# Another order of VectorE's work, and the row maxima split on GpSimd, in a fused attention and FFN kernel

## The reference

```
x  = x + tanh(g_xattn) * attention(layernorm(x), ctx, ctx)      # 16 heads of 16, causal, softmax
x  = x + tanh(g_ffn)   * ffn(layernorm(x))

ffn(t): prob = softmax(t @ w_router + b_router)                 # 16 blocks
        mask = the 4 largest of the 16
        h    = relu(t @ w1.T + b1)                              # 1024 hidden, 64 to a block
        y    = sum over blocks of mask * (h @ w2.T) + b2
```

## Time and profile before

| | |
|---|---|
| median of 3 runs | 725.55 us (723.66 to 728.48) |
| the profiled execution's own time | 723.54 us |
| its span, first to last instruction | 721.8 us |
| busy: TensorE, its weight loads | 686.2 us (95%), 628.9 us (87%) |
| busy: VectorE, ScalarE, GpSimd | 576.3 us (80%), 514.2 us (71%), 512.2 us (71%) |
| iterations 6 to 61 (72.5 to 665.0 us of the span) | 592.5 us |

### The profile page before, as it was taken

One profiled execution on the slowest core, in us unless ns is written; L12 is line 12 of the kernel. 1 busy time (PEld: TensorE's weight loads), 2 busy tenths in 40 slices (PEclk: granted clock), 3 DMA queues, 4 the chain that ended last, 5 costly groups with the idle time before them and its releaser, 6 DMA issues.

```text
span 721.8 us, 30666 instructions
## 1 busy us (share of the span) xinstructions
PE 686.2 (95%) x13072; PEld 628.9 (87%) x13072; DVE 576.3 (80%) x1614; ACT 514.2 (71%) x785; POOL 512.2 (71%) x651
## 2 busy tenths in 40 slices
PE   6869999999999999999999999999999999999888
PEld 5657889998999999889899998989989899899787
DVE  5789988888887888888788888879888888977562
ACT  3656787787777778778777877877787786787532
POOL 3676767778777777877877787777777777765542
PEclk8979999999999999999999999999999999999999
DMA  5313354454345435435544443553454345242010
GB/s 163 99 42 61 75 109 87 86 109 91 77 98 108 89 87 108 86 70 109 108 80 95 109 75 88 102 109 76 98 105 74 88 109 87 59 79 47 20 37 30
DMA packets 161815, 61.91 MB, mean 86 GB/s; under 512 B 135696, under 2 KB 161424, under 8 KB 161680
## 3 DMA queue, kind: packets, MB, share of 16 engines
q1 hardware_dynamic: 160848, 58.38, 38.8%
q10 hardware_dynamic: 832, 1.57, 0.7%
HBM read 19.03 MB, written 8.39 MB: 38 GB/s over the span
## 4 chain that ended last, share of the span: by engine, by line
PE 61%; DVE 24%; issue 5%; ACT 4%; DMA 3%; POOL 2%; SPq 1%; POOLq 0%; ACTq 0%; DVEq 0%
PE bank L414 8%; PE bank L437 6%; PE score_banks L335 6%; PE bank L439 6%; PE bank L438 6%; PE bank L415 6%; PE bank L416 6%; PE score_banks L305 5%; PE bank L348 4%; DVE max_found_in L638 4%; PE bank L362 3%; DVE stats L608 3%; DVE hid L711 2%; DVE q_parts L651 2%; DVE x L666 2%
## 5 line engine op out<-in xcount | busy, mean ns | idle before, releaser
L832 POOL TENSOR_TENSOR h_low<-hid,h_high 128x512 fp32r<-128x512 f32 x128 | 165.2, 1291 | 118.6 <-ACT hid L532 118.4
L825 POOL TENSOR_SCALAR_AFFINE_SELECT weights<-weights 128x1024 f32<-128x1024 f32 x128 | 139.7, 1115 | 56.6 <-ACT weights L510 56.6
L414 PE MATMUL bank<-xT_high,w_high 128*128 128x256 f32 x496 | 151.1, 305 | 8.7 <-DVE hid L711 8.1
L510 ACT ACTIVATE weights<-score_banks 128x1024 f32<-128x1024 f32 x128 | 124.3, 1024 | 45.3 <-PE score_banks L335 45.3
L437 PE MATMUL bank<-w_high,h_high 128*128 128x256 f32 x488 | 142.0, 291 | 4.9 <-DVE y_out L689 4.3
L415 PE MATMUL bank<-xT_low,w_high 128*128 128x256 f32 x496 | 138.8, 280 | 0.0
L416 PE MATMUL bank<-xT_high,w_low 128*128 128x256 f32 x496 | 138.6, 279 | 0.0
L711 DVE SCALAR_TENSOR_TENSOR hid<-bank,b_cols,used_all 128x256 f32<-128x256 f32 x248 | 108.2, 477 | 36.9 <-PE bank L416 36.2
L439 PE MATMUL bank<-w_high,h_low 128*128 128x256 f32 x488 | 136.4, 280 | 0.0
L438 PE MATMUL bank<-w_low,h_high 128*128 128x256 f32 x488 | 136.3, 279 | 0.0
L414 PEld LDWEIGHTS bank<-xT_high,w_high 128*128 128x128 f32 x496 | 93.4, 188 | 19.4 <-DVE hid L711 14.0
(11 more groups left out here) (106 smaller groups left out, 1485.8 us busy)
## 6 DMA issues: line engine op xcount, KB each, us to landing
x_in<-in_x SPq DMA_DIRECT2D x31, 256.0 KB, 3.1
out_y<-y_out SPq DMA_DIRECT2D x31, 256.0 KB, 2.5
c_in<-in_ctx SPq DMA_DIRECT2D x30, 256.0 KB, 3.1
qT<-qT SPq DMA_DIRECT2D x128, 4.0 KB
w_stage<-in_w1T ACTq DMA_DIRECT2D x1, 1024.0 KB, 5.2
hid<-in_w2T SPq DMA_DIRECT2D x8, 128.0 KB, 2.6
kT_parts<-k_parts SPq DMA_TRANSPOSE x57, 3.3
qT_parts<-q_parts SPq DMA_TRANSPOSE x57, 3.3
```

The source lines that it names most:

```text
L414: pe.matmul(out=bank, lhsT=w1_high[:, k, c], rhs=high, start=k == 0, stop=False)
L510: act.activation(weights[:, b % 2, half * 2 * HB:(half + 1) * 2 * HB, :].rearrange("p h q -> p (h q)"), score_banks[:, 2 * half:2 * half + ...
L825: pool.affine_select(out=w, in_=w, compare_op=ALU.is_ge, fill=0.0, base=0, pattern=[[0, 2 * HB], [1, S]], channel_multiplier=-1).then_inc( ...
L832: pool.tensor_tensor(h_low[:, p % 2, chunks], hid[:, n % 4], h_high[:, p % 2, chunks].bitcast(F32), ALU.subtract).then_inc(h_low_made, 1)
```

## The change

- VectorE's order in an iteration: `finished` now ahead of `attention_added`; the mask of the first hidden piece right behind `row_maximum`, ahead of `normalised_again` and `layernorm_stats`.
- The maxima always go to column 20 of `q_pad`. `maximum_parts` on VectorE is gone; GpSimd's `query_parts` copies columns 0 to 20 in place of 0 to 15, waits for the maxima, and runs for the last two carriers too.
- GpSimd's `query_parts` stands behind `key_parts` and the first layernorm's rstd, where it was ahead of both.
- The addition of eps moves from VectorE to GpSimd, twice an iteration, in front of the power.
- SyncE: `max_row` ahead of `used_spread`.
- The three level columns of the high halves are no longer set to constants in `q_parts`; they are copied with the rest.

```diff
             def row_maximum(b):
                 dve.wait_ge(scored, b + 1)
                 carrier = b + MAX_LAG
-                ride = q_pad[:, carrier % QS, :, RIDE_COL] if q_early(carrier) else max_found_in[:]
-                ride = ride.rearrange("p (t g u) -> p u t g", g=2, u=U)
+                if carrier >= N:
+                    dve.wait_ge(q_parts_made, carrier - QS - QUERIES_BY_PE + 1)
+                ride = q_pad[:, carrier % QS, :, RIDE_COL].rearrange("p (t g u) -> p u t g", g=2, u=U)
...
-            def maximum_parts(b):
-                carrier = b + MAX_LAG
-                n, slot = divmod(carrier - QUERIES_BY_PE, 2)
-                dve.wait_ge(max_found, b + 1)
...
-                dve.tensor_copy(q_parts[:, slot, :, :, RIDE_COL],
-                                max_found_in[:].bitcast(U16).rearrange("p (h l) -> p l h", l=2)).then_inc(max_parts_made, 1)
...
             for i in ITERATIONS:                                  # VectorE
                 pr, pu = router_pair(i), used_pair(i)
                 p, m = hidden_pair(i)
+                if 0 <= i - OUT_LAG - 1 < N:
+                    finished(i - OUT_LAG - 1)
                 if 0 <= i - 2 < N:
                     attention_added(i - 2)
-                if 0 <= i - OUT_LAG - 1 < N:
-                    finished(i - OUT_LAG - 1)
                 if 0 <= i + 1 < N:
                     row_maximum(i + 1)
-                    if not q_early(i + 1 + MAX_LAG):
-                        maximum_parts(i + 1)
+                if p is not None:
+                    hidden_masked(p, m)
                 if 0 <= i - 2 < N:
                     normalised_again(i - 2)
                 if 0 <= i + 4 < N:
                     layernorm_stats(i + 4)
-                if p is not None:
-                    hidden_masked(p, m)
...
-            def rstd_of(ve, result, s, b, ve_made, rstd_made):    # GpSimd
+            def rstd_of(mv, ve, result, s, b, mean_made, ve_made, rstd_made):
+                pool.wait_ge(mean_made, b + 1)
+                pool.tensor_scalar(ve[:, s], mv[:, s, 1:2], LN_EPS, None, ALU.add).then_inc(ve_made, 1)
                 pool.wait_ge(ve_made, b + 1)
                 pool.tensor_tensor(result[:, s], ve[:, s], half_power[:], ALU.pow).then_inc(rstd_made, 1)
...
             def query_parts(b):
                 n, slot = divmod(b - QUERIES_BY_PE, 2)
-                pool.wait_ge(qn_made, b + 1)
+                if b < N:
+                    pool.wait_ge(qn_made, b + 1)
+                pool.wait_ge(max_found, b - MAX_LAG + 1)
                 if n >= 1:
                     pool.wait_ge(q_spread[slot], 16 * n)
-                pool.tensor_copy(q_parts[:, slot, :, :, 0:HD],
-                                 q_pad[:, b % QS, :, 0:HD].bitcast(U16).rearrange("p h (d l) -> p l h d", l=2)
+                pool.tensor_copy(q_parts[:, slot, :, :, 0:RIDE_COL + 1],
+                                 q_pad[:, b % QS, :, 0:RIDE_COL + 1].bitcast(U16).rearrange("p h (d l) -> p l h d", l=2)
                                  ).then_inc(q_parts_made, 1)
...
                 elif 0 < i + 3 < N:
                     values(i + 3)
-                if QUERIES_BY_PE <= i + 3 < N:
-                    query_parts(i + 3)
                 if KEYS_BY_PE <= i + 3 < N:
                     key_parts(i + 3)
                 if 0 <= i + 4 < N:
                     if i + 4 == 0:
                         pool.wait_ge(numbers_set, 1)
-                    rstd_of(ve1, rstd1, (i + 4) % 2, i + 4, ve1_made, rstd1_made)
+                    rstd_of(mv1, ve1, rstd1, (i + 4) % 2, i + 4, x_mean, ve1_made, rstd1_made)
+                if QUERIES_BY_PE <= i + 3 < N + MAX_LAG:
+                    query_parts(i + 3)
                 if 0 <= i < N:
                     causal_weights(i)
...
             for i in ITERATIONS:                                  # SyncE
                 pu = used_pair(i)
+                if 0 <= i < N:
+                    max_row(i)
                 if pu is not None:
                     used_spread(pu)
-                if 0 <= i < N:
-                    max_row(i)
                 if QUERIES_BY_PE <= i + 3 < N + MAX_LAG:
                     queries_spread(i + 3)
```

More of the change, by code:

```diff
@@ L30 @@
 ONE_HIGH = 0x3F80
-NEG_HIGH = 0xFC80
 LOAD_AHEAD = 6
@@ L112, in build @@
         kT = sb("kT", [P, TS, BANK], F32)
-        max_found_in = sb("max_found_in", [P, HEADS], F32)
         q_parts = sb("q_parts", [P, 2, 2, HEADS, PAD], U16)
@@ L180, in build @@
         x2_stats, x2_mean, xn_made = sem("x2_stats"), sem("x2_mean"), sem("xn_made")
-        ve1_made, ve2_made, max_parts_made = sem("ve1_made"), sem("ve2_made"), sem("max_parts_made")
+        ve1_made, ve2_made = sem("ve1_made"), sem("ve2_made")
         xT_low_made, hid_made, y_made = (sem(n) for n in ("xT_low_made", "hid_made", "y_made"))
@@ L196, in build @@
             "parts_zeroed", "parts_ones_set", "parts_levels_set", "k_parts_made"))
-        q_parts_zeroed, q_parts_ready, q_parts_made = (sem(n) for n in (
-            "q_parts_zeroed", "q_parts_ready", "q_parts_made"))
+        q_parts_zeroed, q_parts_made = sem("q_parts_zeroed"), sem("q_parts_made")
         w_low_made, h_low_made = sem("w_low_made"), sem("h_low_made")
@@ L605, in places, with stats_of @@
                                 ident16[rows, rows].unsqueeze(1).to_broadcast([PAD, U, PAD])).then_inc(place_made, 1)
-            def stats_of(source, stats, mv, ve, s, b, stats_made, mean_made, ve_made):
+            def stats_of(source, stats, mv, s, b, stats_made, mean_made):
                 dve.bn_stats(stats[:, s, :], source).then_inc(stats_made, 1)
@@ L610, in stats_of @@
                 dve.bn_aggr(mv[:, s, :], stats[:, s, :]).then_inc(mean_made, 1)
-                dve.wait_ge(mean_made, b + 1)
-                dve.tensor_scalar(ve[:, s], mv[:, s, 1:2], LN_EPS, None, ALU.add).then_inc(ve_made, 1)
             def layernorm_stats(b):
@@ L619, in layernorm_stats @@
                     dve.wait_ge(x_landed[slot], 16 * (n + 1))
-                stats_of(x_in[:, b % XS, :], stats1, mv1, ve1, b % 2, b, x_stats, x_mean, ve1_made)
+                stats_of(x_in[:, b % XS, :], stats1, mv1, b % 2, b, x_stats, x_mean)
             def normalised(b):
@@ L668, in attention_added @@
                 dve.wait_ge(x2_made, b + 1)
-                stats_of(x2[:, s], stats2, mv2, ve2, s, b, x2_stats, x2_mean, ve2_made)
+                stats_of(x2[:, s], stats2, mv2, s, b, x2_stats, x2_mean)
             def normalised_again(b):
@@ L864, in _ @@
                     b = i - 2
-                    rstd_of(ve2, rstd2, b % 2, b, ve2_made, rstd2_made)
+                    rstd_of(mv2, ve2, rstd2, b % 2, b, x2_mean, ve2_made, rstd2_made)
                     if b == 0:
@@ L890, in _ @@
                                     ).then_inc(parts_levels_set, 1)
[L891 to L895, removed]
+                    pool.memset(q_parts[:, :, :, :, RIDE_COL + 1:], 0).then_inc(q_parts_zeroed, 1)
                 if p is not None:
@@ L928, in queries_spread @@
                     sync.wait_ge(q_copied, b - 1)
-                if b < N:
-                    sync.wait_ge(q_parts_made, b - QUERIES_BY_PE + 1)
-                sync.wait_ge(max_parts_made, b - QUERIES_BY_PE + 1)
+                else:
+                    sync.wait_ge(q_parts_zeroed, 1)
+                sync.wait_ge(q_parts_made, b - QUERIES_BY_PE + 1)
                 sync.dma_start_transpose(qT_parts[:, slot].rearrange("p l (r s) -> p (l r) s", s=S),
```

## The result

The changed kernel takes 796.03 us (793.95 to 798.09, 4 runs) against 725.85: ratio 1.0965, 95% interval 1.0916 to 1.1015. The prediction was 796. Its profiled execution took 798.09 us with a span of 796.2.

What follows compares the result with a forecast made beforehand. TensorE was taken to set the pace at 10.58 us an iteration; the change makes a loop through GpSimd, SyncE and ScalarE 6.78 + 1.74 + 3.5 = 12.02 us. Over 53 turns 76 us, less 3: 796 us, range 758 to 832.

Steps and rivals of the forecast that it cites:

- the circle: GpSimd's query split, SyncE's transpose, ScalarE's join and last Relu, GpSimd's L832, next split: 12.02 us a turn against 10.58.
- The signs: Expected profile marks: ScalarE waits before the join 1 to 2 us each, 60 to 100 in all; TensorE idle some 15%.
- The terms: GpSimd work entering the stretch from L832 to the query transpose: 0.57 + 0.52 + 0.17 + 0.48 = 1.74 us.
- Key split: GpSimd's splitting of the keys, now ahead of the query split: 0.57 us more in each turn.
- power: GpSimd's operation for rstd1, now ahead of the query split: 0.52 us more in each turn.
- The copy: GpSimd's query split copying 21 columns for 16: 0.17 us more, low end 0.13.
- The additions: Two epsilon additions moved to GpSimd: 0.24 us each, 0.48 for both, ends 0.2 and 1.2.
- fixed part: Time from one query split to the next less the transfer: 6.78 us before plus 1.74, constant near 8.5.
- the transfer's: Landing of the queries' transpose, from its issue to ScalarE's join: mean put at 3.5 us, shortest taken as 3.0.
- SyncE's queue and the mask: Maxima's transfers ahead of the choice's transpose: worth 5.8 us of TensorE's waits; later choice holds the mask under 1 us.
- VectorE's order: Mask starts about 2.4 us earlier, xn behind it has room: worth TensorE's 12.5 us of mask waits while TensorE sets pace.
- The rival on the other side: Query split's delay is covered because joined tiles are used over an iteration later: faster, 706 us, chance 0.05.

Runs made afterwards that it cites:

- split_early: Changed kernel with GpSimd's query split moved back ahead of the key split and rstd1: 716.2 us, ratio 0.989 to the kernel before.
- split_late_only: Kernel before with only GpSimd's query split moved behind the key split and rstd1, no work added: 779.94 us, ratio 1.077.
- join_last_sync_back: Changed kernel with ScalarE's join of the queries at the end of its iteration and SyncE's old order: 729.69 us, ratio 1.007.
- sync_back: Changed kernel with only SyncE's old order, the choice's transpose ahead of the maxima: 798.4 us, ratio 1.101.
- order_only: Kernel before with VectorE's and SyncE's new orders, GpSimd untouched: 709.96 us, ratio 0.980.
- order_aligned_sync_back: Kernel before with VectorE's new order, SyncE's old order and max_found_in declared last: 703.38 us, ratio 0.972.
- early_ve_back: Changed kernel with the query split ahead of key split and rstd1, and both epsilon additions on VectorE: 706.44 us, ratio 0.977.
- spare_64: Changed kernel with an unused tensor of 64 bytes a partition declared in front of q_parts: 825.78 us, ratio 1.138.
- before_aligned: Kernel before with the 64-byte max_found_in declared last: 723.69 us, ratio 1.000.

## Why the prediction was right

**The bound and the circle: right.** The pace of the splits was forecast at 12.02 us and is 11.87; the join waits in 56 of 57 turns. The part of the turn without transfer was to be constant near 8.5: it is 8.47 in the turns without the choice and 9.36 in those with it (6.54 and 6.93 before), so it isn't constant. Of the 0.89 between them 0.4 is the choice, the rest a wait of which I tell below. Moving the one step either way (split_early, split_late_only) and opening the circle elsewhere (join_last_sync_back) show it as the cause, and not only as a fitting story.

**The signs: some were off.** ScalarE's wait for the queries was to be 1 to 2 us a turn, 60 to 100 in all; it is 3.1 and 175.5. The forecast is about the time added to the turns (1.44 us each). But ScalarE's waits for TensorE shrank by 93 us (in front of `oT` from 71.2 to 12.9, of `logitT` from 47.3 to 12.2), and the idle time gathered in front of the join. TensorE is idle for 12% of the stretch (589.24 of 668 us busy), not 15, and what it waits for most is xn (66.1 us), then the maxima (37.7). The granted clock there fell from 1.00 to 0.98; TensorE isn't in the turn.

**The terms: errors that cancelled.** Key split 0.58 and power 0.52 (0.57 and 0.52 forecast), from this timeline of GpSimd in the changed kernel:

```profile
451.95 0.21 POOL L776 TENSOR_SCALAR ve<-mv 128x1 f32<-128x1 f32 x1
452.25 0.57 POOL L778 TENSOR_TENSOR rstd<-ve,half_power 128x1 f32<-128x1 f32 x1
...
453.86 0.61 POOL L793 COPY k_parts<-c_in 128x512 uint16<-128x512 uint16 x1
454.44 0.38 POOL L776 TENSOR_SCALAR ve<-mv 128x1 f32<-128x1 f32 x1
454.91 0.57 POOL L778 TENSOR_TENSOR rstd<-ve,half_power 128x1 f32<-128x1 f32 x1
455.43 0.75 POOL L804 COPY q_parts<-q_pad 128x672 uint16<-128x672 uint16 x1
```

The copy grew to 0.75, so by 0.08 and not 0.17. The additions take 0.30 and 0.47 to the power's start, 0.77 for 0.48. Added up that is 1.95 for the forecast 1.74, and the turns without the choice grew by 1.93. The fixed part's mean was 8.92 for 8.52, and the transfer's 2.97 for 3.5. The second difference is the 64 bytes, which no row of the kernel before could show: 2.7 is below the 3.0 that I had taken as the shortest landing. With the address as before the same kernel takes 825.8, 30 us above the forecast and still in its range. The turn came out 0.15 below its forecast, 8 us over 56 steps; that I counted 53 turns and took 3 us off, where 56 turns were paid, made up for 7 of these. So the circle was read rightly, and that the time was met to the microsecond is luck. The estimate of 0.72 for the additions, worked out from the Trainium skill, "GPSIMD Engine Reference", section "Elementwise — side-by-side cycle accounting", came nearer to the 0.77 than mine; the addition itself has a mean of 277 ns in this trace for VectorE's 154, 1.8 times, though the page's 1.96 is measured on two inputs of 2048 columns.

**SyncE's queue and the mask: wrong.** The prediction had the choice's later landing hold up the mask "by under 1 us", still in time for TensorE, and valued the swap at 5.8 us. In the changed kernel the mask waits 2.7 us a time (76.3 over 28). The swap is the small part of that, as the two orders show, the changed kernel first, then sync_back:

```profile
435.42 1.38 ACT L495 COPY qT<-qT_parts 128x1024 uint16<-128x1024 uint16 x1 [3.01 <-DMA qT_parts<-q_parts]
436.66 0.50 ACT L538 ACTIVATE used<-marked,minus_one 128x256 bf16<-128x256 f32 x1
...
436.82 1.15 SPq L904 DMA_DIRECT2D qT<-qT  x2
438.07 1.20 SPq L944 DMA_TRANSPOSE used_all<-used  x1
...
440.44 0.88 DVE L696 SCALAR_TENSOR_TENSOR hid<-bank,b_cols,used_all 128x256 f32<-128x256 f32 x2 [1.79 <-issue]
```

```profile
438.49 0.51 ACT L538 ACTIVATE used<-marked,minus_one 128x256 bf16<-128x256 f32 x1
...
439.09 1.17 SPq L944 DMA_TRANSPOSE used_all<-used  x1
...
442.20 0.88 DVE L696 SCALAR_TENSOR_TENSOR hid<-bank,b_cols,used_all 128x256 f32<-128x256 f32 x2 [1.70 <-issue]
```

From the choice's start to the mask's it is 3.78 us in the one and 3.71 in the other. Over 27 choices the transpose is issued 1.2 us behind the choice's end with the new order and 0.2 with the old, but with the old it is longer on its way, and the mask still waits 2.5 us a time (70.7 over 28). What the prediction left out is the choice's own place: ScalarE makes it behind the join, and it waits for its input only twice (the last line of the waits in the result). Moved ahead, the mask reaches for a choice that the circle has delayed. The wait goes on into the circle: mask, xn, statistics, rstd1, split; GpSimd waits for those statistics 0.57 us on the mean of the turns with a choice and under 0.1 in the others, which is the rest of the 9.36. In the fast version the swap costs 5.4 us.

**VectorE's order: right in sign, too small.** order_only gives 14 us by it, the swap's cost included; without the swap, 20 (order_aligned_sync_back). That is more than the 12.5 us of the waits for the mask; where the rest comes from wasn't tried. The forecast said that xn, pushed behind the mask, "has the room". TensorE waits for it 66.1 us in the changed kernel, partly because xn itself waits there for rstd2 (38.2 us, 30 times), but also 24.2 us in order_only and 9.2 in order_aligned_sync_back, so the room was not quite enough.

**The rival on the other side** (706 us, the split has cover) would have needed L819 not to wait for the join. It was the right question: where the split comes early again, in split_early and early_ve_back, the time is 716 and 706.

## What to carry to other kernels

Follow a step through all queues until it comes back to its own engine, add up the turn, and compare it with the pace; here 0.5 us of room in 10.6 was the whole margin, and an engine busy for 71% of the time could not take about 2 us more at that point, while in split_early it took 49 us more work than before with a gain. A step's place in an in-order queue is priced by what stands behind it when its input is late, and a step moved forward needs its inputs forward too: the mask was moved, the choice was not. Once a turn is the bound, everything in it is paid in full, also the long landings that had fallen into the room.

## What the runs showed that I had not expected

The landing of the queries' DMA transpose (256 KB within SBUF) depends here on where the tiles lie: 64 bytes a partition in front of them turn 2.7 us into 3.2 (changed kernel and spare_64; 3.3 and 2.7 in the kernel before and before_aligned). Which of the shifted tiles matters wasn't tried.

VectorE's step with two inputs from SBUF (L651, the residual) has a mean of 1064 ns in the changed kernel; the same step took 520 before (L666). GpSimd and VectorE in the changed kernel:

```profile
446.42 1.54 POOL L819 TENSOR_TENSOR h_low<-hid,h_high 128x512 fp32r<-128x512 f32 x1
...
458.31 1.28 POOL L819 TENSOR_TENSOR h_low<-hid,h_high 128x512 fp32r<-128x512 f32 x1
```

```profile
446.33 0.48 DVE L651 SCALAR_TENSOR_TENSOR x<-att,tanh_g,x_in 128x256 f32<-128x256 f32 x1
...
458.44 1.43 DVE L651 SCALAR_TENSOR_TENSOR x<-att,tanh_g,x_in 128x256 f32<-128x256 f32 x1
```

Where VectorE starts first, GpSimd's operation takes 1.54 for 1.28; where GpSimd starts first, VectorE's takes 1.43 for 0.48 and ends 0.28 us behind it. The Trainium skill, "GPSIMD Engine Reference", section "Specifications", has the two share an interface to SBUF when VectorE reads two inputs there; these rows agree. What it costs the kernel no run here shows.
